# Three edits to a sixteen-layer kernel: quarter-array PV, a maximum from a copy, encoder products issued last

## The chip, the cores and the metric

The kernel runs on one core of a Trainium2 chip. The metric is device time in microseconds for the whole program, lower is better. TensorE is written PE, VectorE DVE, ScalarE ACT, GpSimd POOL and SyncE SP.

## The reference, cut to what matters

The input is 8 batches of 256 tokens with 128 features. Sixteen residual layers run one after the other, `x = x + layer(layernorm(x))`. The layers that the change touches are:

- layers 1 and 3, routed attention. Four groups times eight batches give 32 units. A router picks for each unit 128 query tokens and 64 key tokens. Eight heads of 64 features attend over the 64 keys and one learned null key with its null value; the result is projected to 128 features, weighted by the query's gate and added back at the tokens it came from.

```python
scores = q @ k.T * 64 ** -0.5            # 128 queries x (64 keys + the null key), 8 heads
p = softmax(scores)
out = (p[:, :64] @ v + p[:, 64] * v_null) @ w_out
```

- layers 2 (causal), 10 (no mask) and 14 (window of 64, with an output projection): attention with 16 heads of 8 features over 256 tokens, `softmax(q @ k.T * scale) @ v`.
- layers 13 and 15: a mixture of encoders. Two of four encoders are picked per batch, so each layer has 16 units. A unit is the same 16-head attention, a projection, a layer norm, a feed-forward of 128 to 512 to 128, and a second layer norm.

All matmuls of these layers are in float32.

## The kernel before, in words

Each layer is a stage with its own buffers and semaphores. Each engine runs one program written out in steps, in order, and semaphores tie the engines together.

**Routed stage** (`routed_attention_stage`, tiles `s1a_...` and `s3a_...`). A first part sorts the router's logits; its length is set by VectorE's top-k loop. Then step `i` works on unit `i` and finishes older units. TensorE issues in step `i`: the scores of unit `i` (`S`, L3259), the items of `RoutedPlan`, four turns of the probabilities of unit `i-1` (`PT`, L3270), PV of `i-2` (`OT`, L3282), the projection of `i-3` (`OUT`, L3293, and L3296 for the null value), and the scatter of `i-4` (`X`, L3305). The items are the value product of unit `i` (`v`, L3234), in three steps of four the front of the next group (gather: two items, L3212 and L3214; queries: four items, L3219; keys: two items, L3227), and the turn of the null probability of `i-1` (`pn`, L3241). All items write one ring of two banks, `F`:

```python
n = plan.number[it]
f = F[:, n % 2, :]
if n >= 2:
    pe.wait_ge(f_cp, n - 1)
```

so an item waits until the item two places before it has been copied out. ScalarE copies every item (the values at L3342, scaled by the gate), then takes the exponential of unit `i` (L3346), then copies `PT` and `OT`. VectorE's step is: maximum (L3412), subtraction (L3416), after the exponential the row sum (L3420) and reciprocal (L3423), then the copy of `OUT` (L3429), two additions into `x` from the scatter (L3446), and the placement matrix (L3405). POOL multiplies by the reciprocal and issues the indirect DMAs.

**Slot stages** (`slot_attention_stage`, and the same helpers in `encoder_stage`). `SlotPlan` gives 32 (or, in an encoder stage, 64) steps of four heads each. Scores are computed twice, once to find the row maxima and once turned, with the maximum subtracted in the product. Six PSUM banks in three pairs (`R`) rotate: the turned scores of step `u` overwrite the pair in which the first two heads' scores of step `u+1` stand, so they wait until VectorE has taken those maxima. TensorE's step `u` is: scores of `u+1` (L471), early items, PV of the step before (L520; two steps before with a mask), turned scores of `u` (L500), turns of the maxima of `u+1` (L534), turn of the output (L543), late items. The scores of `u+2` wait for the first exponential of `u` (L569), which needs the turned scores. Other products of the unit (queries and keys `qk`, values `v`, layer norm's turn `h`, and in the encoders `t`, `y`, `t1`, `f1`, `f2`, `f3`) share one bank `X` and are spread over four steps by two tables:

```python
early = {0: [("qk", 1)], 1: [("f1", -2)], 2: [("y", -1)], 3: [("f3", -2)]}
late = {0: [("t1", -2)], 1: [("t", -1)], 2: [("f2", -2)], 3: [("v", 1)]}
```

`qk` of the next unit is sent through DRAM (L409 store, L415 four loads) and must be back for the scores of the next unit's first step, issued in the fourth step of this one. SP's queue issues these and the loads of the encoders' weights in order.

## Time and profile before

| | |
|---|---|
| three runs | 3067.08, 3072.36, 3075.82 us; median 3072.36 |
| the profiled execution | 3062.8 us, its span 3061.1 us |
| mean granted clock of TensorE | 0.951 of full speed |
| busy share of the span | PE 88%, PE weight loads 59%, DVE 62%, ACT 45%, POOL 36% |
| routed stages, steady part | 397 to 622 and 860 to 1085 us |
| slot stages | 641 to 795 (causal), 1475 to 1641 (no mask), 2492 to 2637 us (window) |
| encoder stages | 2078 to 2450 and 2655 to 3040 us |

A stage is the stretch between the first and the last of its attention steps. In a timeline of TensorE the start of a row less the start of the row before is what the instructions of the row before cost; the busy time of a row includes the last matmul's run-out. float32 matmuls appear as two instructions each.

### The profile page before, as it was taken

The page shows a single profiled execution, that of the slowest core. Times are in us where ns is not written, and L with a number is a line of the kernel's source. Part 1 is how long each engine was busy: PE and PEld are TensorE (multiplying, and loading weights), DVE is VectorE, ACT ScalarE, POOL GpSimd, SP SyncE. Part 2 cuts the span into 40 slices and gives each one's busy share as a digit, 9 for nine tenths or more (in the row PEclk, how much of TensorE's full clock was granted, in tenths as well). Part 3 has the DMA queues.
Part 4 walks back from the last instruction along what each step waited for, and adds up shares of the span by engine and source line. Part 5 has one row for each costly group of instructions (what it writes and reads, how often), then busy time and mean ns, then how long its engine had stood idle before and what let it go on. Part 6 is the DMA issues. An engine that isn't in the chain of part 4 may idle for free. (4 is left out here: it accounts for less than half of the span.)

```text
span 3061.1 us, 62358 instructions
## 1 busy us (share of the span) xinstructions
PE 2707.2 (88%) x24181; PEld 1791.2 (59%) x24181; DVE 1910.4 (62%) x4325; ACT 1389.4 (45%) x2900; POOL 1094.8 (36%) x1448
## 2 busy tenths in 40 slices
PE   7899699978799977888788899997999989789997
PEld 2344367756467755566455677774666657456664
DVE  7888644556544566743675577765677746566764
ACT  5556144434244434423453355543555534355553
POOL 4788444324344323313112334330222246312222
PEclk9899799999789988988999999998999999999999
DMA  2000200001000001010111000002222201112221
GB/s 82 1 1 1 78 19 19 9 24 31 22 19 20 10 1 36 18 69 26 39 26 34 17 1 1 1 1 72 59 83 75 72 19 30 61 46 75 80 74 47
DMA packets 62498, 107.09 MB, mean 35 GB/s; under 512 B 8138, under 2 KB 47062, under 8 KB 61440
## 3 DMA queue, kind: packets, MB, share of 16 engines
q1 hardware_dynamic: 56832, 94.63, 10.3%
q0 software_dynamic: 5376, 8.47, 1.0%
q8 instruction: 197, 3.23, 0.4%
q14 instruction: 93, 0.76, 0.1%
HBM read 79.66 MB, written 23.86 MB: 34 GB/s over the span
## 5 line engine op out<-in xcount | busy, mean ns | idle before, releaser
L569 ACT ACTIVATE s_sT<-s_R 128x1024 f32<-128x1024 f32 (+2 forms) x448 | 415.6, 947 | 157.7 <-PE s_R L500 157.5
L604 DVE TENSOR_REDUCE s_negm<-s_R 128x4 f32<-128x1024 f32 x320 | 376.8, 1220 | 86.6 <-PE s_R L471 84.4
L471 PE MATMUL s_R<-s_qk 32*128 32x256 f32 (+2 forms) x3584 | 241.8, 382 | 92.2 <-ACT s_sT L569 66.8
L500 PE MATMUL s_R<-s_qA,s_qk 32*128 32x256 f32 (+2 forms) x3584 | 241.0, 382 | 20.9 <-DVE s_negm L604 12.6
L622 DVE TENSOR_TENSOR s_qA<-s_qk,s_OB 128x256 f32<-128x256 f32 x224 | 94.3, 421 | 264.6 <-PE s_OB L543 257.9
L471 PEld LDWEIGHTS s_R<-s_qk 32*128 32x128 f32 x3584 | 159.3, 185 | 142.6 <-issue 122.3
L520 PE MATMUL s_OB<-s_sT,s_v 128*32 128x256 f32 (+2 forms) x3584 | 224.5, 368 | 10.2 <-ACT s_sT L569 6.4
L500 PEld LDWEIGHTS s_R<-s_qA,s_qk 32*128 32x128 f32 x3584 | 163.2, 185 | 106.1 <-issue 102.8
L576 ACT ACTIVATE s_oc<-s_OB 128x256 f32<-128x256 f32 x224 | 85.8, 383 | 268.6 <-PE s_OB L520 264.3
L1519 POOL TENSOR_TENSOR s_pr<-s_pr,s_rinv 128x1024 f32<-128x1024 f32 x64 | 121.1, 1892 | 186.7 <-DVE s_rinv L1630 186.7
L2860 POOL TENSOR_TENSOR all_hT<-s0s_hs,s0s_cb 128x1024 f32<-128x1024 f32 x64 | 150.6, 2353 | 29.2 <-PE s0s_Y L2807 13.8
L520 PEld LDWEIGHTS s_OB<-s_sT,s_v 128*32 128x32 f32 x3584 | 94.1, 109 | 96.0 <-issue 33.2
L2886 DVE TENSOR_TENSOR_SCAN s0s_hs<-s0s_dA,s0s_dBu 128x1024 f32<-128x1024 f32 x64 | 146.1, 2283 | 0.9 <-POOL s0s_dBu L2848 0.9
L609 DVE TENSOR_REDUCE s_negm<-s_R 128x2 f32<-128x256 f32 (+2 forms) x256 | 116.4, 518 | 45.3 <-PE s_R L481 45.0
L585 POOL TENSOR_SCALAR_AFFINE_SELECT s_sT<-s_sT 128x512 f32<-128x512 f32 x128 | 81.2, 634 | 159.6 <-ACT s_sT L569 157.9
L2807 PE MATMUL s0s_Y<-all_hT,all_ident 128*128 128x512 f32 x256 | 125.2, 612 | 2.4 <-POOL all_hT L2860 2.4
L1195 POOL TENSOR_TENSOR s_veps<-s_mv,all_eps 128x2 f32<-128x2 f32 x64 | 16.6, 260 | 303.5 <-DVE s_mv L1403 303.5
L1603 ACT ACTIVATE s_pr<-s_S,s_negmax 128x256 f32<-128x256 f32 x256 | 117.4, 478 | 4.1 <-DVE s_negmax L1633 4.1
L534 PE MATMUL s_OB<-all_ident,s_negm 128*128 128x128 f32 x448 | 98.0, 300 | 2.8 <-DVE s_negm L604 2.5
L1633 DVE TENSOR_REDUCE s_negmax<-s_S 128x4 f32<-128x1024 f32 x64 | 78.3, 1223 | 29.5 <-PE s_S L1539 29.4
L1645 DVE COPY s_prT<-s_PT 128x1024 f32<-128x1024 f32 x64 | 78.3, 1224 | 22.8 <-PE s_PT L1568 22.8
L1611 ACT ACTIVATE s_v<-s_O 128x256 f32<-128x256 f32 x64 | 24.6, 384 | 147.1 <-PE s_O L1557 147.1
(613 smaller groups left out, 6263.0 us busy)
## 6 DMA issues: line engine op xcount, KB each, us to landing
s_wB<-enc_b SPq DMA_DIRECT2D x32, 962.5 KB, 4.8
s_scratch<-s_pk SPq DMA_DIRECT2D x58, 256.0 KB, 2.0
s_qk<-s_scratch SPq DMA_DIRECT2D x232, 64.0 KB
s_wA<-enc_a SPq DMA_DIRECT2D x32, 193.0 KB, 4.2
big<-moe SPq DMA_DIRECT2D x2, 2347.0 KB, 10.8
all_W<-weights SPq DMA_DIRECT2D x2, 2199.5 KB, 13.5
big<-routed SPq DMA_DIRECT2D x2, 2084.0 KB
s_returned<-s_back SPq DMA_DIRECT2D x2, 1024.0 KB
```

The lines of the kernel that those rows point to most:

```text
L471: last = pe.matmul(S[h][:, t * T:t * T + hi - lo], b.qk[rows, r % 2, 0, c, t * P:(t + 1) * P], b.qk[rows, r % 2, 1, c, lo:hi], start=(t == ...
L500: last = pe.matmul(b.R[:, a.turned_at(u, h // 2), :][:, h % 2, a.at(kt)], b.qk[rows, r % 2, 1, c, kt * P:(kt + 1) * P], b.qA[rows, u % 2, ...
L520: last = pe.matmul(b.OB[32 * h:32 * (h + 1), lo:hi], b.v[:, r % 2, kt, a.HP * c + h, :], b.sT[:, j % (a.lag + 1), h, a.at(kt)], start=(kt ...
L534: last = pe.transpose(b.OB[:, T + t * P:T + (t + 1) * P], b.negm[:, u % 2, t, :], g.ident[:])
L569: act.activation(b.sT[:, u % (a.lag + 1), 2 * p:2 * p + 2, 0:a.width], b.R[:, a.turned_at(u, p), 0:a.width], ACT.Exp).then_inc(s.expd, 1)
L604: ins = dve.tensor_reduce(b.negm[:, u % 2, :, at].rearrange("p t h -> p h t"), S.rearrange("p h (t k) -> p h t k", t=TT), AX_X, ALU.max, n ...
L609: ins = dve.tensor_reduce(b.negm[:, u % 2, t, at], S[:, :, t * T:t * T + hi - lo], AX_X, ALU.max, negate=True)
L1519: pool.tensor_tensor(p, p, rinv[:, u % 3, :, :].rearrange("p h t -> p (h t)").unsqueeze(2) .to_broadcast([P, 2 * TT, T]), ALU.mult).then_i ...
L1603: ins = act.activation(pr[:, u % 3, h, t, :], S[:, u % 2, h, t * T:(t + 1) * T], ACT.Exp, bias=negmax[:, u % 3, h, t:t + 1], accum_out=sum ...
L2807: last = pe.matmul(Y[:, m, :], g.ident[:], hc[:, j % 2, m, :], start=False, stop=(j % N == N - 1), skip_group_check=True)
L2860: pool.tensor_tensor(hc[:, q % 2, :, :], hs[:, q % 2, :, :], cb[:, q % 2, :].unsqueeze(1).to_broadcast([P, M, C]), ALU.mult)\
L2886: dve.tensor_tensor_scan(out=hs[:, q % 2, :, :].rearrange("p m c -> p (m c)"), data0=dA[:, q % 2, :, :].rearrange("p m c -> p (m c)"), dat ...
```

## The change

Three edits, of which the first has several parts.

1. Routed stages. PV alternates over the four 64x64 quarters of the array, with the output in two banks, where it used the two diagonal quarters. Values are stored less the null value, `v - v_null`, and the null value's projection is added once per query as a constant row (`nw`) when `OUT` is taken out; the turn of the null probability, its copy, its POOL product and the 8-row matmul L3296 go. The values' copy moves from ScalarE to VectorE, between the subtraction and the row sum. `OUT` and `X` share one bank, and the scatter is issued before the projection.
2. Slot stages (layers 2, 10, 14), `hold=True`. ScalarE copies the second head's scores to SBUF (`kept`); VectorE takes the maxima of head 0 from PSUM, of heads 2 and 3 from PSUM, of head 1 from the copy. The turned scores wait for head 0's maximum and the copy.
3. Encoder stages. Items move between the tables, early items are issued after PV, and ScalarE does the late items' copies after both exponentials.

```diff
-    early = {0: [("qk", 1)], 1: [("f1", -2)], 2: [("y", -1)], 3: [("f3", -2)]}
-    late = {0: [("t1", -2)], 1: [("t", -1)], 2: [("f2", -2)], 3: [("v", 1)]}
+    early = {0: [("t1", -2)], 1: [("t", -1)], 2: [("y", -1)], 3: [("v", 1)]}
+    late = {0: [("qk", 1)], 1: [("f1", -2)], 2: [("f2", -2)], 3: [("f3", -2)]}
...
                     if u + 1 < U:
                         slot_scores_pe(pe, g, a, b, u + 1)
+                    if 0 <= u - a.lag < U:
+                        slot_pv_pe(pe, a, b, u - a.lag)
                     for item in a.early(u):
                         other(item)
-                    if 0 <= u - a.lag < U:
-                        slot_pv_pe(pe, a, b, u - a.lag)
...
+                    if 0 <= u - a.lag < U:
+                        slot_out_act(act, a, b, u - a.lag)
                     for item in a.early(u):
                         other(item)
-                    if 0 <= u - a.lag < U:
-                        slot_out_act(act, a, b, u - a.lag)
                     if 0 <= u < U:
                         slot_exp_act(act, a, b, u, 0)
+                        slot_exp_act(act, a, b, u, 1)
                     for item in a.late(u):
                         other(item)
-                    if 0 <= u < U:
-                        slot_exp_act(act, a, b, u, 1)
```

In the encoders VectorE's addition of `f3` moves with its item to the end of the step. The slot stages:

```diff
+def slot_hold_act(act, a, b, u):
+    s = b.sems
+    act.wait_ge(s.scored, 2 * u + 1)
+    if u:
+        act.wait_ge(s.maxed, a.maxima * u)
+    act.activation(b.kept[:, 0:a.key_width], b.R[:, a.scores_at(u, 0), :][:, 1, 0:a.key_width], ACT.Copy)\
+       .then_inc(s.held, 1)
...
+def slot_max_dve(dve, a, b, u):
+    s = b.sems
+    pairs = [b.R[:, a.scores_at(u, p), :] for p in range(2)]
+    dve.wait_ge(s.scored, 2 * u + 1)
+    if a.maxima == 3:
+        slot_maxima_of(dve, a, b, u, (0,), pairs[0][:, 0:1, :]).then_inc(s.maxed, 1)
     else:
+        slot_maxima_of(dve, a, b, u, (0, 1), pairs[0]).then_inc(s.maxed, 1)
+    dve.wait_ge(s.scored, 2 * u + 2)
+    slot_maxima_of(dve, a, b, u, (2, 3), pairs[1]).then_inc(s.maxed, 1)
+    if a.maxima == 3:
+        dve.wait_ge(s.held, u + 1)
+        slot_maxima_of(dve, a, b, u, (1,), b.kept[:].unsqueeze(1)).then_inc(s.maxed, 1)
...
     if u + 1 < a.U:
-        pe.wait_ge(s.maxed, 2 * (u + 1) + 1)
+        pe.wait_ge(s.maxed, a.maxima * (u + 1) + 1)
+        if a.maxima == 3:
+            pe.wait_ge(s.held, u + 2)
...
                 for u in a.steps:
+                    if u + 1 < U:
+                        slot_hold_act(act, a, b, u + 1)
                     for item in a.early(u):
```

The routed stages:

```diff
-            if 0 <= i - 1 < self.UNITS:
-                items.append(("turn", i - 1))
...
                         if n >= 2:
-                            pe.wait_ge(f_cp, n - 1)
+                            old = plan.order[n - 2]
+                            if old[0] == "v":
+                                pe.wait_ge(v_cp, old[1] + 1)
+                            else:
+                                pe.wait_ge(f_cp, plan.copies[old] + 1)
...
                             for h in range(H):
-                                rows = slice((h % 2) * DH, (h % 2 + 1) * DH)
-                                c = h // 2
-                                last = pe.matmul(OT[rows, c * P:(c + 1) * P], v[rows, j % 3, c * DH:(c + 1) * DH],
+                                half, c = h % 2, h // 2
+                                rows, to = slice(half * DH, (half + 1) * DH), half ^ (c % 2)
+                                last = pe.matmul(OT[to * DH:(to + 1) * DH, c % 2, (c // 2) * P:(c // 2 + 1) * P],
+                                                 v[rows, j % 3, c * DH:(c + 1) * DH],
                                                  prT[rows, j % 2, c * P:(c + 1) * P], start=True, stop=True,
-                                                 skip_group_check=True)
+                                                 skip_group_check=True, tile_position=(half * DH, to * DH))
...
+                        j = i - 3
+                        if 0 <= j < U:
+                            s = plan.unit(j)[0]
+                            pe.wait_ge(oT_cp, j + 1)
+                            if j >= 1:
+                                pe.wait_ge(o_cp, j)
+                            if j >= 2:
+                                pe.wait_ge(added, TT * (j - 1))
...
+                    def values(u):
+                        n, s, c = plan.number[("v", u)], plan.unit(u)[0], columns(u)[1]
+                        dve.wait_ge(f_mm, n + 1)
+                        dve.scalar_tensor_tensor(out=v[:, u % 3, :], in0=F[:, n % 2, 0:256], scalar=sig[:, 1, c:c + 1],
+                                                 in1=g.big("r_nvb")[:, s * 256:(s + 1) * 256], op0=ALU.mult,
+                                                 op1=ALU.subtract).then_inc(v_cp, 1)
...
                                               ALU.subtract).then_inc(shifted, 1)
+                            values(i)
                             dve.wait_ge(expd, i + 1)
...
-                            dve.tensor_copy(o[:, j % 2, :], OUT[:, 0:D]).then_inc(o_cp, 1)
+                            dve.tensor_tensor(o[:, j % 2, :], OUT, nw[:, plan.unit(j)[0], :], ALU.add)\
+                               .then_inc(o_cp, 1)
...
                             dve.wait_ge(scattered, j + 1)
+                            dve.wait_ge(projected, min(j + 2, U))
```

The packed weights of the routed layers gain `r_nvb` (1024 columns) and `r_nvc` (16) and lose `r_nvT` (128); `nw` has 128 equal rows in place of one row per head.

## Rows read from the trace of the kernel before

**Rows 1.** Busy time by stage: routed (first), slot without mask, second encoder.

```profile
397.00:622.00 225.00, 222.51 (x1908) 161.82 (x1904) 121.72 (x296) 101.73 (x216) 92.95 (x128) 0.98 0.05 15
...
1475.00:1641.00 166.00, 137.20 (x1732) 84.85 (x1725) 115.32 (x234) 84.12 (x122) 22.05 (x40) 1.00 0.10 25
...
2655.00:3040.00 385.00, 349.89 (x3956) 232.28 (x3956) 250.45 (x549) 203.44 (x342) 89.24 (x151) 0.99 0.23 71
```

**Rows 2.** Timeline of TensorE, one routed step and the next.

```profile
481.94 1.11 PE L3259 MATMUL s1a_S<-s1a_kT,s1a_qT 64*128 64x65 f32 x16
...
483.56 0.33 PE L3212 MATMUL s1a_F<-all_ident,s_hq 128*128 128x128 f32 x1
...
484.21 0.33 PE L3212 MATMUL s1a_F<-all_ident,s_hq 128*128 128x128 f32 x1
...
485.44 1.09 PE L3282 MATMUL s1a_OT<-s1a_prT,s1a_v 64*64 64x128 f32 x16
...
486.46 1.16 PE L3293 MATMUL s1a_OUT<-big,s1a_oT 128*128 128x128 f32 x8
...
487.55 0.48 PE L3296 MATMUL s1a_OUT<-s_nw,s1a_pnT 8*128 8x128 f32 x2
...
488.60 1.11 PE L3259 MATMUL s1a_S<-s1a_kT,s1a_qT 64*128 64x65 f32 x16
...
490.23 3.80 PE L3219 MATMUL s1a_F<-s1a_sel,big 128*128 128x512 f32 x8
```

**Rows 3.** Timeline of TensorE, causal slot stage.

```profile
692.14 0.86 PE L520 MATMUL s_OB<-s_sT,s_v 128*32 128x256 f32 x16
...
692.93 0.94 PE L500 MATMUL s_R<-s_qA,s_qk 32*128 32x256 f32 x16
```

**Rows 4.** Timeline of VectorE, routed step.

```profile
488.07 0.29 DVE L3429 COPY s1a_o<-s1a_OUT 128x128 f32<-128x128 f32 x1 [1.19 <-PE s1a_OUT L3296]
...
488.78 0.61 DVE L3446 SCALAR_TENSOR_TENSOR all_x<-s1a_X,s_rcount,all_x 128x128 f32<-128x128 f32 x2 [0.42 <-PE s1a_X L3305]
...
489.76 0.70 DVE L3412 TENSOR_REDUCE s1a_mx<-s1a_S 128x8 f32<-128x520 f32 x1
...
490.50 0.70 DVE L3416 TENSOR_TENSOR s1a_ev<-s1a_S,s1a_mx 128x520 f32<-128x520 f32 x1
```

**Rows 5.** Waits in the routed stage, 450 to 550 us.

```profile
PEld s1a_F L3212 <- ACT s1a_v L3342: 0.9, 4, 0.2
```

**Rows 6.** Timeline, slot stage without mask, one plain step.

```profile
1554.29 1.15 PE L471 MATMUL s_R<-s_qk 32*128 32x256 f32 x16 [0.61 <-ACT s_sT L569]
...
1555.36 1.07 PE L520 MATMUL s_OB<-s_sT,s_v 128*32 128x256 f32 x16
...
1555.62 2.33 DVE L604 TENSOR_REDUCE s_negm<-s_R 128x4 f32<-128x1024 f32 x2
...
1556.95 1.15 PE L500 MATMUL s_R<-s_qA,s_qk 32*128 32x256 f32 x16 [0.52 <-DVE s_negm L604]
...
1559.29 1.15 PE L471 MATMUL s_R<-s_qk 32*128 32x256 f32 x16 [0.39 <-ACT s_sT L569]
```

**Rows 7.** Timeline of TensorE, first encoder, scores of four steps.

```profile
2231.67 1.15 PE L471 MATMUL s_R<-s_qk 32*128 32x256 f32 x16 [0.40 <-ACT s_sT L569]
...
2237.16 1.15 PE L471 MATMUL s_R<-s_qk 32*128 32x256 f32 x16 [0.40 <-ACT s_sT L569]
...
2240.95 0.44 PE L534 MATMUL s_OB<-all_ident,s_negm 128*128 128x128 f32 x2
...
2242.41 1.15 PE L471 MATMUL s_R<-s_qk 32*128 32x256 f32 x16
...
2248.81 1.15 PE L471 MATMUL s_R<-s_qk 32*128 32x256 f32 x16 [0.17 <-ACT s_sT L569]
```

**Rows 8.** Timeline of SyncE's queue, first encoder.

```profile
2229.34 0.33 SPq L409 DMA_DIRECT2D s_scratch<-s_pk  x1
```

**Rows 9.** DMA share and GB/s in a half microsecond.

```profile
2236.50:2237.00 0.50, 1.00 0.03 2
```

More of the change, by code:

```diff
@@ L188, with __init__ @@
     QUERIES = {None: ((0, 256), (0, 256)), "causal": ((0, 256), (128, 256)), "window": ((0, 192), (128, 256))}
-    def __init__(self, units, early, late, extra, mask=None, first=()):
+    def __init__(self, units, early, late, extra, mask=None, first=(), hold=False):
         self.units, self.U, self.mask = units, units * self.NC, mask
         self.lag = 1 if mask is None else 2
+        self.maxima = 3 if hold else 2
         self.steps = range(-1, self.U + extra)
@@ L470, in slot_scores_pe @@
             rows = slice(32 * h, 32 * (h + 1))
-            last = pe.matmul(S[h][:, t * T:t * T + hi - lo], b.qk[rows, r % 2, 0, c, t * P:(t + 1) * P],
+            last = pe.matmul(S[h][:, a.keys_at(t)], b.qk[rows, r % 2, 0, c, t * P:(t + 1) * P],
                              b.qk[rows, r % 2, 1, c, lo:hi], start=(t == 0), stop=(a.mask is None and t == TT - 1),
@@ L643, in slot_attention_stage @@
         early[3], late[2] = [("y", -1)], [("t", -1)]
-    a = SlotPlan(B, early, late, 4, mask, [("h", 0), ("qk", 0), ("v", 0), ("h", 1)])
+    a = SlotPlan(B, early, late, 4, mask, [("h", 0), ("qk", 0), ("v", 0), ("h", 1)], hold=True)
     U, NC = a.U, a.NC
@@ L767, in _ @@
                     if u + 1 < U:
-                        for p in range(2):
-                            slot_max_dve(dve, a, b, u + 1, p)
+                        slot_max_dve(dve, a, b, u + 1)
                     for item in a.early(u):
@@ L1408, in _ @@
                     if u + 1 < U:
[L1409 to L1410 removed]
+                        slot_max_dve(dve, a, b, u + 1)
                     for item in a.early(u):
@@ L1460, in _ @@
                                                  op1=ALU.add).then_inc(unit_done, 1)
+                    for item in a.late(u):
+                        what, r = item
+                        if what == "f3":
+                            dve.wait_ge(x1b_ready, r + 1)
+                            if r:
+                                dve.wait_ge(unit_done, r)
+                            dve.wait_ge(s.x_mm, a.number[item] + 1)
+                            dve.tensor_tensor(r2[:], b.X[:, 0:T].rearrange("p (t n) -> p t n", t=TT),
+                                              x1b[:, r % 2, :, :], ALU.add).then_inc(r2_ready, 1)
+                            dve.wait_ge(r2_ready, r + 1)
+                            dve.sem_inc(s.x_used, 1)
                     if (r := at_step(u, 3, -3)) is not None and r % 2 and r // 2 < leave:
@@ L2936, in __init__ @@
                     items += self.front(nxt, ("gather", "q", "k")[i % self.NB - 1])
-            if 0 <= i - 1 < self.UNITS:
-                items.append(("turn", i - 1))
             self.steps.append(items)
-        self.number = {item: n for n, item in enumerate(item for s in self.steps for item in s)}
+        self.order = [item for s in self.steps for item in s]
+        self.number = {item: n for n, item in enumerate(self.order)}
+        self.copies = {item: n for n, item in enumerate(item for item in self.order if item[0] != "v")}
     @staticmethod
@@ L3185, in copied @@
             def copied(*item):
-                return plan.number[item] + 1
+                return plan.copies[item] + 1
             with nc.Block() as block:
@@ L3305, in _ @@
                                 last = pe.matmul(X[:, h * D:(h + 1) * D], sqT[:, j % 4, h * P:(h + 1) * P],
-                                                 o[:, j % 2, :], start=True, stop=True)
+                                                 o[:, j % 2, :], start=True, stop=True, skip_group_check=True)
                             last.then_inc(scattered, 1)
+                        j = i - 3
[6 more added lines that the diff above has]
+                                pe.wait_ge(added, TT * (j - 1))
+                            for c in range(4):
+                                at = (c % 2) * T + (c // 2) * P
+                                last = pe.matmul(OUT, oT[:, j % 2, at:at + P], wo[:, (4 * s + c) * P:(4 * s + c + 1) * P],
+                                                 start=(c == 0), stop=(c == 3), skip_group_check=True)
+                            last.then_inc(projected, 1)
                 @block.scalar
```

119 lines of the change are left out of this document (44 added, 75 removed).

## Prediction, written before the change was run

> **What bounds the kernel now.** I read the busy table by stage first. The change touches seven of sixteen stages, about 1700 of 3061 us. In the routed stages PE is busy 222.5 of 225 us at a granted clock of 0.98, DVE only 121.7 [rows 1]: every microsecond taken from PE's program there is a microsecond, until another engine is late. The slot stage without a mask is different: PE 137 and DVE 115 of 166 us, so no engine is full, and a loop of waits sets the step. The encoder has PE 350 of 385 us. Next I read PE's timeline of one routed step, start to start [rows 2], and the same of VectorE [rows 4]. For the loops I read one plain slot step with its waits [rows 6] and the starts of the scores over the steps of an encoder unit [rows 7].
>
> **Routed stages: what PE loses.** 32 units in each of two stages.
> - PV: 16 instructions from 485.44 to 486.46, 1.02 us [rows 2]. Two quarters work at a time, so these are eight groups of two. The 16 instructions at L3219 take 3.80/8 = 0.475 us for 512 columns with the run-out, some 0.11 us per 128 columns, and eight groups at 0.11 plus the entry are the 1.02. With four quarters there are four groups: 0.44 us less per unit, if all four run together. No row shows quarters mixed this way. Bounds: 0, if a quarter in the same rows has to wait, and 0.44. Four slices in one direction do run together: in the causal stage 16 PV instructions, half of them of 256 columns, go by in 0.79 us, 49 ns each [rows 3], against 107 ns and more for one alone. I take 0.44.
> - The Trainium skill, page "TensorE: Matmul & The Clock Gate", section "Wait — 56ns, not 53.3ns?", speaks against this: with instructions decoded by the sequencer each matmul costs about 62 ns however short. 16 times that is the 1.0 us of today, and the quarters would save nothing. The 49 ns of the causal row lie below it, so the trace disagrees and I keep the full term.
> - The turn of the null probability is one instruction of 128 columns: 0.11 us.
> - From the first projection to the next scores now: 488.60 - 486.46 = 2.14 us: eight full instructions with a slow entry and exit (1.09), the 8-row pair (0.41), the scatter's four with another entry (0.64). The new order has twelve full instructions with one entry and exit: 1.09 + 4 x 0.11 = 1.53. That is 0.60 us less.
> - Together 1.15 us per unit, 64 units: **-74 us**.
>
> **Routed stages: what comes back.** The values' copy is now behind VectorE's maximum and subtraction, and an item waits for the copy of the one two before it. Today ScalarE frees the values' bank in time: 0.9 us of such waits in 100 us, at most 0.2 [rows 5]. After the change:
> - The maximum starts 1.16 us after the first score matmul today (489.76 - 488.60). `OUT` is now the last thing before the scores. Its taking out started 0.31 us after the last matmul of its group (488.07 against 487.76), which is 0.11 after the next scores start. Then 0.29 for it, and 0.98 from the first addition to the maximum [rows 4]: the maximum starts at 1.38.
> - Subtraction at 1.38 + 0.74, its end 0.70 later, values about 0.45 (nearest rows: 0.41 for L3405's kind, a 256-column operation; I take a little more for two inputs), a hop of 0.05: bank free at 3.32.
> - The second gather item could start at 484.21 - 481.94 = 2.27, the second query item at 1.62 + 0.95 = 2.57, the second key item at about 2.5. Waits: 1.05, 0.75, 0.80; 2.6 us in a group of four, seven groups, two stages: +36. In the first eight steps VectorE has two more additions of 0.3 behind it: +4. Bounds: 0, should the copy not be late, and 1 us more per wait (42 waits, +42) should VectorE run behind. I take **+40**.
> - VectorE itself: 121.7/32 = 3.8 us per unit plus 0.45. The shortest step (no front) is 6.66 less two gather items of 0.65, 5.36; it becomes 4.2. VectorE's 4.25 just reaches it: +1.
> - ScalarE loses 0.47 + 0.25 us per unit, POOL a product of 0.2. Neither is late today, so nothing. The copy of `OUT` becomes an addition of the same size, 0. The load grows by 912 columns, 0.47 MB; it lies under the top-k loop, and without that cover it would be 1 to 2 us.
> - Net **-33 us**.
>
> **Slot stages.** In a plain step the turned scores start 1556.95 - 1554.29 = 2.66 us after the scores, having waited 0.52 for VectorE; the next scores follow 2.34 later [rows 6]. The two-head maximum takes 1.17 (2.33 for two). One of 520 elements takes 0.70 [rows 4], and ScalarE's copy, which takes part beside it, about 0.6. So the wait falls to the end of PV, 1.07 + 1.0 = 2.07, and the step from 5.0 (4.88 where no layer norm stands before it) to 4.4: 0.5 us. But only one step in four can use it: with an item ahead of PV the turned scores were not waiting for VectorE, and in the fourth step the turns of the maxima, now 0.1 us later because three reduces take 2.45 instead of 2.33, with `h` behind them fill the gap. 8 x 0.5 = 4. With masks the maxima are shorter: 8 x 0.35 and 8 x 0.3. **-9 us**; if the copy gains nothing and all 96 steps get 0.1 longer, +10.
>
> **Encoders.** Two steps in four now take 5.49 us (2237.16 - 2231.67), the third 5.25, the fourth 6.40 [rows 7]. All have a product between scores and turned scores, and then 2.3 us to the next scores in which PE rests 0.4 at the least [rows 7]. Behind the turned scores a product fills that rest, and it needs no change of array shape. `f2` shows the price: 2242.41 - 2240.95 = 1.46 from the maxima's turns to the next scores with a late product of four instructions of 256 columns. The first two steps get the maxima's turns at 3.7 (2.66 + 1.08) and a late `qk` or `f1` of the same size: 3.7 + 1.46 = 5.16, -0.33 each. The third keeps its pair, 0. The fourth has `v` early and `f3` late, 16 instructions of 0.11 instead of four of 0.22: 3.79 + 1.46 + 0.9 = 6.15, -0.25. That is 0.91 us per unit, 14 units with all items, two stages: -25; in the first encoder the next layer's norm work makes VectorE late in every other unit, +2. **-23 us**.
> - `qk` of the next unit moves from some 3 us into the first step to about 6.7: turned scores, two exponentials and then the copies, which ScalarE now does last. From the store's issue to the end of the loads is 7.4 to 7.7 us (2229.34 to 2236.5 or 2237.0) [rows 8, 9], so the data is there at 14.3, and the scores want it at 5.16 + 5.16 + 5.25 = 15.6. It is hidden with 1.3 us to spare. SP's queue holds the loads of the next weights behind it; they aren't wanted for a unit.
>
> **Sum.** -33 - 9 - 23 = **-65 us**. The profiled execution, 3062.8 us (span 3061.1), would become 2998. It lies 10 us below the median of the runs; from the median, 3072.4 - 65 = **3007 us**.
>
> **Rivals.**
> - The quarters run in pairs (bound 0): 64 x 0.44 = 28 us come back, 3035. For it: no row shows them. Against it: [rows 3].
> - The values' copy isn't late: VectorE takes it earlier than I think, all 40 us stay, 2967. Against it: its place in VectorE's program behind two operations of 0.7 us.
> - VectorE runs behind: `OUT` is now taken out at the end, and each wait is 0.7 us longer: 42 x 0.7 = +29, 3036. For it: 4.25 us of work against 4.2.
> - `qk` lands late: one microsecond in 28 units, 3035. For it: only 1.3 us to spare, and weights loads start while it lands.
> - The other side: the same wait behind VectorE becomes the routed stages' bound. To undo 65 us it must be 65/42 = 1.55 us longer than my 0.95; at 2.2 the time is 3100. It would take VectorE being a whole half step behind. Against it: query and key steps give VectorE 2 to 4 us to catch up.
>
> **How the numbers follow.** Forecast 0.48; quarters in pairs 0.12; copy not late 0.10; VectorE behind 0.11; `qk` late 0.09; two or three of these together, back to where it was, 0.05; the other side 0.05. A measurement of this kernel can't tell 0.3%, 9 us, from no change. Faster 0.90, same 0.05, slower 0.05. The range runs from the copy that isn't late to beyond the single rivals near 3035, to 3045, with 2970 below. The forecast's own range is 2990 to 3022.
>
> **What would show it.** Right: PV's 16 instructions in 0.6 us; from the first scatter to the next scores 1.53; the second item of each front waiting 0.7 to 1.1 us for VectorE's new values line, the largest new wait on PE; the short routed step near 4.3 us, the gather step near 5.5 plus its wait; plain slot steps of 4.4; encoder steps of 5.16, 5.16, 5.25 and 6.15. Wrong: PV still about 1 us, a wait of the scores for the loads of `qk`, gaps of PE before the probabilities' turns, or a lower granted clock where PE now rests.

## The result, and the profile after

The changed kernel took 3016.09 us (median, 3015.27 to 3018.5) beside 3073.15 for the kernel before on the same chip: a ratio of 0.9818, 95% interval 0.9801 to 0.9835, 57 us between the medians. The forecast was 3007 (range 2970 to 3045). The two profiled executions differ by 44 us only (3062.8 and 3018.5, spans 3061.1 and 3016.8). The 13 us between are the choice of executions: the one of before lies 10 us below its median, that of the changed kernel 2 above. Single profiles differ in parts that no edit touches as well: the stretch from the last scores of the second routed stage to the first of the slot stage without a mask took 405.6 us in the profile of before, 413.5 in that of after, and 404 to 412 in the experiments. The steady steps repeat to 0.01 us from profile to profile.

The busy times of the changed kernel's page:

```profile
PE 2647.1 (88%) x23955; PEld 1745.4 (58%) x23989; DVE 1944.5 (64%) x4549; ACT 1397.8 (46%) x2868; POOL 1086.0 (36%) x1384
```

Its timeline of TensorE, the same routed steps as [rows 2]:

```profile
486.03 0.33 PE L3248 MATMUL s1a_F<-all_ident,s_hq 128*128 128x128 f32 x1 [0.76 <-DVE s1a_v L3438]
...
487.05 0.67 PE L3316 MATMUL s1a_OT<-s1a_prT,s1a_v 64*64 64x128 f32 x16
487.65 0.71 PE L3328 MATMUL s1a_OX<-s1a_o,s1a_sqT 128*128 128x128 f32 x4
488.20 1.06 PE L3341 MATMUL s1a_OX<-big,s1a_oT 128*128 128x128 f32 x8
489.18 1.11 PE L3291 MATMUL s1a_S<-s1a_kT,s1a_qT 64*128 64x65 f32 x16
...
490.80 1.13 PE L3255 MATMUL s1a_F<-s1a_sel,big 128*128 128x512 f32 x2
492.22 2.94 PE L3255 MATMUL s1a_F<-s1a_sel,big 128*128 128x512 f32 x6 [0.29 <-DVE s1a_v L3438]
```

PV takes 0.60 us to the next row, where [rows 2] have 1.02, and from the scatter to the next scores it is 489.18 - 487.65 = 1.53, where it was 2.14. The second gather item waits 0.76 us for VectorE's values. The changed kernel's waits from 450 to 550 us (us in total, times, longest), as [rows 5]:

```profile
PEld s1a_F L3248 <- DVE s1a_v L3438: 4.7, 4, 1.7
...
PEld s1a_F L3255 <- DVE s1a_v L3438: 4.5, 4, 1.1
...
PEld s1a_F L3263 <- DVE s1a_v L3438: 2.1, 3, 0.7
```

Its timeline of VectorE in the gather step, as [rows 4]:

```profile
484.15 0.70 DVE L3446 TENSOR_REDUCE s1a_mx<-s1a_S 128x8 f32<-128x520 f32 x1
484.88 0.70 DVE L3450 TENSOR_TENSOR s1a_ev<-s1a_S,s1a_mx 128x520 f32<-128x520 f32 x1
485.50 0.47 DVE L3438 SCALAR_TENSOR_TENSOR s1a_v<-s1a_F,s_sig,big 128x256 f32<-128x256 f32 x1
```

The maximum starts 1.16 us after the scores and the values' copy 0.62 after the subtraction; the bank is free at about 486.0. The first eight steps look different. TensorE in the early gather step of the changed kernel:

```profile
426.35 1.11 PE L3291 MATMUL s1a_S<-s1a_kT,s1a_qT 64*128 64x65 f32 x16
...
431.22 0.47 PE L3248 MATMUL s1a_F<-all_ident,s_hq 128*128 128x128 f32 x1 [2.59 <-DVE s1a_v L3438]
...
432.12 1.06 PE L3303 MATMUL s1a_PT<-all_ident,s1a_pr 128*128 128x128 f32 x4
433.12 1.13 PE L3316 MATMUL s1a_OT<-s1a_prT,s1a_v 64*64 64x128 f32 x16
```

VectorE in the same step:

```profile
427.06 1.53 DVE L3469 SCALAR_TENSOR_TENSOR all_x<-all_W,s_missed,all_x 128x128 f32<-128x128 f32 x2
428.51 0.60 DVE L3483 SCALAR_TENSOR_TENSOR all_x<-s1a_OX,s_rcount,all_x 128x128 f32<-128x128 f32 x2
...
430.69 0.48 DVE L3438 SCALAR_TENSOR_TENSOR s1a_v<-s1a_F,s_sig,big 128x256 f32<-128x256 f32 x1
```

POOL beside it, the product of the probabilities with the reciprocal:

```profile
427.07 1.04 POOL L3415 TENSOR_TENSOR s1a_pr<-s1a_ev,s1a_rsum 128x512 f32<-128x512 f32 x1 [1.14 <-DVE s1a_rsum L3458]
```

Busy times and granted clock (the third value from the right) while it waits, right after, over the rest of the step and in the next:

```profile
428.70:431.20 2.50, 0.00 (x0) 0.00 (x0) 2.43 (x6) 0.46 (x1) 1.64 (x2) 0.94 0.09 26
431.20:432.20 1.00, 0.98 (x5) 0.98 (x6) 0.00 (x0) 0.00 (x0) 0.00 (x0) 0.50 0.21 66
432.20:435.70 3.50, 3.50 (x33) 2.78 (x31) 0.90 (x2) 2.10 (x4) 1.10 (x2) 0.70 0.02 5
435.80:437.30 1.50, 1.50 (x21) 1.13 (x20) 1.42 (x6) 0.00 (x0) 1.20 (x2) 1.00 0.00 0
```

The additions of the null token take 1.53 us for two ahead of the maximum, the values' copy starts 430.69 - 426.35 = 4.34 us after the scores, and the gather item waits 2.59. The first of the two additions alone takes 1.20 us, and it ends 0.15 after POOL's product (428.11); where no product of POOL runs beside them they take 0.33 to 0.41 each. Near the end of the wait TensorE's granted clock fell to half, for 3.4 us: the turns of the probabilities took 1.06 us in place of 0.60, PV 1.13 in place of 0.67.

TensorE's timeline of a plain slot step after the change (compare [rows 6]):

```profile
1522.00 1.15 PE L481 MATMUL s_R<-s_qk 32*128 32x256 f32 x16 [0.61 <-ACT s_sT L581]
...
1524.12 1.15 PE L512 MATMUL s_R<-s_qA,s_qk 32*128 32x256 f32 x16
...
1526.45 1.15 PE L481 MATMUL s_R<-s_qk 32*128 32x256 f32 x16 [0.16 <-ACT s_sT L581]
```

And the scores of an encoder unit (compare [rows 7]):

```profile
2201.47 1.15 PE L481 MATMUL s_R<-s_qk 32*128 32x256 f32 x16
...
2206.55 1.15 PE L481 MATMUL s_R<-s_qk 32*128 32x256 f32 x16
...
2211.64 1.15 PE L481 MATMUL s_R<-s_qk 32*128 32x256 f32 x16
...
2216.88 1.15 PE L481 MATMUL s_R<-s_qk 32*128 32x256 f32 x16
...
2223.05 1.15 PE L481 MATMUL s_R<-s_qk 32*128 32x256 f32 x16
```

The plain step fell from 4.88 or 5.0 to 4.45; the turned scores start 2.12 us after the scores (2.66 before). The encoder's steps are 5.08, 5.09, 5.24 and 6.17, a sum of 21.58 where it was 22.63. But in some units the scores wait for `qk`. SyncE's queue for a good unit (compare [rows 8]):

```profile
2208.12 0.33 SPq L419 DMA_DIRECT2D s_scratch<-s_pk  x1
2210.14 2.85 SPq L425 DMA_DIRECT2D s_qk<-s_scratch  x4
```

The same for a bad one:

```profile
2384.23 0.33 SPq L419 DMA_DIRECT2D s_scratch<-s_pk  x1
2387.84 2.84 SPq L425 DMA_DIRECT2D s_qk<-s_scratch  x4
```

And its scores on TensorE:

```profile
2394.69 1.15 PE L481 MATMUL s_R<-s_qk 32*128 32x256 f32 x16 [1.64 <-DMA s_qk<-s_scratch]
```

The loads are issued when the store has completed: 2.02 us after it in the one, 3.61 in the other. There the scores wait 1.64. The DMA view shows an instruction fetch beside the slow store (packets, MB, share; then KB and us to landing):

```profile
q8 instruction: 1, 0.02, 2.5%
...
s_scratch<-s_pk SPq DMA_DIRECT2D x1, 256.0 KB, 3.6
```

Beside the fast one it shows none:

```profile
s_scratch<-s_pk SPq DMA_DIRECT2D x1, 256.0 KB, 2.0
```

Stage by stage, from the first scores to the last in the profiles (us):

| stage | before | after | measured | forecast |
|---|---|---|---|---|
| routed, layers 1 and 3 | 210.7, 210.1 | 198.6, 199.3 | -12.1, -10.8 | -33 for both |
| causal slot | 142.3 | 138.7 | -3.6 | -3 |
| slot without mask | 155.9 | 149.3 | -6.6 | -4 |
| window slot | 132.1 | 134.8 | +2.7 | -2 |
| encoders, layers 13 and 15 | 360.7, 357.7 | 354.5, 348.7 | -6.2, -9.0 | -23 for both |

The seven stages add up to 46 us less, near the 44 by which the two profiled executions differ, and not the 57 of the medians.

### The profile page after: what moved, and what is told of

Same layout as the page of the kernel before. It is cut to its first block and busy times, and to the rows that moved or that the text cites. A ratio compares the mean times of both kernels' runs of the same rounds, so it can differ in the third digit from the quotient of the medians.

```text
span 3016.8 us, 62251 instructions
## 1 busy us (share of the span) xinstructions
PE 2647.1 (88%) x23955; PEld 1745.4 (58%) x23989; DVE 1944.5 (64%) x4549; ACT 1397.8 (46%) x2868; POOL 1086.0 (36%) x1384
## 3 DMA queue, kind: packets, MB, share of 16 engines
q0 software_dynamic: 5376, 8.47, 1.0%
## 5 line engine op out<-in xcount | busy, mean ns | idle before, releaser
L581 ACT ACTIVATE s_sT<-s_R 128x1024 f32<-128x1024 f32 (+2 forms) x448 | 402.8, 945 | 187.0 <-PE s_R L512 186.8
L623 DVE TENSOR_REDUCE s_negm<-s_R 128x4 f32<-128x1024 f32 (+1 forms) x320 | 359.5, 1166 | 102.5 <-PE s_R L481 101.2
L627 DVE TENSOR_REDUCE s_negm<-s_R 128x1 f32<-128x128 f32 (+5 forms) x256 | 92.8, 425 | 41.8 <-PE s_R L491 41.5
L546 PEld LDWEIGHTS s_OB<-all_ident,s_negm 128*128 128x128 f32 x448 | 45.1, 141 | 83.0 <-DVE s_negm L623 60.8
## 6 DMA issues: line engine op xcount, KB each, us to landing
big<-moe SPq DMA_DIRECT2D x2, 2347.0 KB, 10.8
```

The source lines that it names most:

```text
L546: last = pe.transpose(b.OB[:, T + t * P:T + (t + 1) * P], b.negm[:, u % 2, t, :], g.ident[:])
L581: act.activation(b.sT[:, u % (a.lag + 1), 2 * p:2 * p + 2, 0:a.width], b.R[:, a.turned_at(u, p), 0:a.width], ACT.Exp).then_inc(s.expd, 1)
L623: return dve.tensor_reduce(b.negm[:, u % 2, :, at].rearrange("p t h -> p h t"), S[:, :, 0:a.key_width].rearrange("p h (t k) -> p h t k", t ...
```

## The experiments

Each kernel's ratio is to the kernel before, run on the same chip; the changed kernel's is 0.9818. Differences between two kernels are differences of their ratios, times 3070 us. Stage times are those of one profile for each kernel. Twelve kernels ran.

**pairs.** PV on the two diagonal quarters again, the rest as changed (the order of the projection's packed weights and of the null values follows, not shown).

```diff
-half, c = h % 2, h // 2
-rows, to = slice(half * DH, (half + 1) * DH), half ^ (c % 2)
+rows, to = slice(half * DH, (half + 1) * DH), half
```

> The changed kernel with each product of PV back on the two diagonal quarters of the array (rows and columns of the same half), the projection's weights and the null values in the order that fits; everything else stays, the two output banks too. My theory, four quarters work side by side: PV's 16 instructions go from 0.60 us back to about 1.0, the steps of the routed stages get 0.4 us longer, and the time is 64 x 0.44 = 28 us longer (20 to 30). The rival, that the quarters run in pairs and PV became shorter by something else (the second bank, the order): PV stays at 0.60 us and the time within 3 us.

3030.17 us, 0.9867 (0.9849 to 0.9886): 15 us slower than the changed kernel. Its timeline:

```profile
487.77 1.09 PE L3316 MATMUL s1a_OT<-s1a_prT,s1a_v 64*64 64x128 f32 x16
488.79 0.71 PE L3328 MATMUL s1a_OX<-s1a_o,s1a_sqT 128*128 128x128 f32 x4
```

PV is back at 1.02 us. Every steady step is 0.42 us longer (4.34 to 4.76, 6.19 to 6.62, 8.47 to 8.90, 6.67 to 7.09), the two stages 10.9 and 9.9. The whole time misses the 20 to 30 us that were expected, and is 6 us nearer to the changed kernel than these two stages say; in this profile the stretch of 413.5 us named above took 407.8, the window stage 3.9 us less and the encoders 5.5 more. Parts outside the edit differ by such amounts from profile to profile. In the routed steps the rival is out: with both banks kept, PV took 1.02 us on two quarters and 0.60 on four.

**nulls.** The null token's additions behind the values' copy, under the exponential.

```diff
                             values(i)
+                            if i < B:
+                                for t in range(TT * i, TT * i + TT):
...
                             dve.wait_ge(expd, i + 1)
...
-                        if i < B:
-                            for t in range(TT * i, TT * i + TT):
...
```

> The changed kernel with the two additions of the null token (first eight steps of each routed stage) moved on VectorE from ahead of the next maximum to behind the values' copy, where VectorE otherwise waits for the exponential. Theory: in the changed kernel they take 1.4 us of each early step and hold up the maximum and the values' copy behind it, so that the second item of a front waits 1.8 to 2.6 us where it waits 0.7 later on, and after such a wait PE runs for a while at the lower clock. Moved, the early gather step falls from 9.4 us to 6.2, the other early steps by 0.5 to 2.5, some 7 us for each of two stages: 14 us faster in all. Rival, that the early steps are long for another reason (the gathers' transfers arriving, the softmax starting from nothing): within 3 us, and the early gather step stays at 9.4.

2995.80 us, 0.9755 (0.9739 to 0.9772), 19 us faster than the changed kernel. The routed stages took 192.1 and 191.8 us (6.5 and 7.5 less); the early gather step fell from 9.42 to 6.35, and no steady step changed. The expected 14 us are there; the other 5 lie outside these stages. The edit did two things at once. The additions left VectorE's way to the values' copy, and they left the place beside POOL's product. VectorE in the early gather step:

```profile
425.07 0.61 DVE L3457 SCALAR_TENSOR_TENSOR all_x<-all_W,s_missed,all_x 128x128 f32<-128x128 f32 x2
```

The 32 additions of both stages took 11.0 us together, in the changed kernel 20.1. No run moved the one without the other, so how the 14 us divide between the order and the 9 us of slower additions isn't shown.

**mid.** The values' copy between maximum and subtraction.

```diff
 dve.tensor_reduce(mx[:, i % 2, :, :], s4, AX_X, ALU.max).then_inc(maxed, 1)
+values(i)
 dve.wait_ge(maxed, i + 1)
 ...
-values(i)
 dve.wait_ge(expd, i + 1)
```

> The changed kernel with the values' copy placed between the maximum and the subtraction on VectorE instead of behind both. Theory: the bank comes free 0.7 us earlier, which is the whole wait of the second items of the fronts (0.69 us for a gather, 0.56 for q and k, in steady steps), so some 12 us in the steady steps of both stages and as much again in the first eight, 15 to 25 us faster. The softmax starts 0.47 us later, which costs nothing as long as the probabilities are there for their turns in the next step. Rival: the later softmax makes PE wait ahead of the probabilities' turns in the short steps (4.34 us), 0.3 to 0.5 us in most of 64 steps, which eats the gain: between 5 us faster and 15 slower.

2988.38 us, 0.9737 (0.9716 to 0.9758), 25 us faster than the changed kernel. The stages took 187.6 us each (11.0 and 11.7 less). The steady steps fell from 6.19, 8.47, 6.67 to 5.63, 7.92, 6.12, the short one stayed at 4.34. The early gather step stayed at 9.11: that one belongs to nulls. The later softmax cost nothing in the steady steps; the first step of a stage grew from 2.74 to 3.00.

**both.** The two edits together.

> The changed kernel with both edits of VectorE's program in the routed stages: the values' copy between maximum and subtraction, and the two additions of the null token behind the subtraction, under the exponential. Alone the first made a routed stage 11.4 us shorter than in the changed kernel and the second 7.0. Theory: they take away different waits (the steady ones of the second front items, and those of the first eight steps), but in the first eight steps they overlap by the 0.55 us of each steady wait, 2 to 3 us in a stage: 30 to 36 us faster than the changed kernel in all, a stage of 182 to 184 us, and an early gather step of about 5.7 us. Rival, that the early steps then wait for the probabilities or for the gathers' transfers: no more than the first edit alone, 24 us, and an early gather step that stays above 8.

2974.02 us, 0.9695 (0.9673 to 0.9717), 38 us faster than the changed kernel; the stages took 180.7 and 181.0, 17.9 and 18.3 less, nearly the sum of the two. The early gather step is 5.73 us long:

```profile
424.87 0.33 PE L3248 MATMUL s1a_F<-all_ident,s_hq 128*128 128x128 f32 x1 [0.29 <-DVE s1a_v L3438]
...
425.37 0.60 PE L3303 MATMUL s1a_PT<-all_ident,s1a_pr 128*128 128x128 f32 x4
```

**routed_only.** The kernel before with the routed part alone.

> The kernel before with the routed stages' part of the change alone; encoders as before and no copied head in the slots. My sum had 33 us for it (74 less on PE, 40 back in waits, 1 for VectorE). The profile of the changed kernel shows its two routed stages 12.1 and 10.8 us shorter: 23 us. Theory: 0.9925 of the kernel before (0.990 to 0.995). Rival, that the change gains outside the stages' steps as well (the values' and weights' loads, the front): 0.989 or less.

3043.90 us, 0.9921 (0.9906 to 0.9936): 24 us faster than before. The stages took 198.6 and 199.3 us, as in the changed kernel.

**enc_only.** The kernel before with the encoders' part alone.

> The kernel before with the encoders' part of the change alone (the long products behind the turned scores, both exponentials together); the routed stages and the slot stages as before the change. My sum had 23 us for it; the steady steps of the changed kernel show 1.05 us per unit, 29 us for 28 units, less the waits for the loads of qk, 9 us in its profile, and less some 3 us in the first steps. Theory: 12 to 20 us faster than the kernel before, and waits of the scores for the loads of qk as in the changed kernel. Rival, that these waits come from elsewhere (another stage's edit shifting the transfers): none of them here, and 23 us or more faster.

3039.89 us, 0.9904 (0.9877 to 0.9931): 29.5 us faster than before, more than I expected, with an interval from 21 to 38. Its profile shows 349.8 and 353.5 us for the encoders, 15.1 less than before, with steps of 5.08, 5.08, 5.25 and 6.17 and many waits for the loads of `qk`. Much of the difference is again which executions were profiled: the one of enc_only lies 6.5 us above its median, that of before 7 below the median of the runs beside it, and the two differ by 16. Between the profile's 15 and the median's 29 the runs do not decide, nor between the theory and the rival's 23 or more, though the waits for the loads, which the rival would have gone, are there.

**qbetween.** ScalarE copies `qk` between the two exponentials; the products stay late.

```diff
                         slot_exp_act(act, a, b, u, 0)
+                    copied = [item for item in a.late(u) if item[0] == "qk"]
+                    for item in copied:
+                        other(item)
+                    if 0 <= u < U:
                         slot_exp_act(act, a, b, u, 1)
                     for item in a.late(u):
-                        other(item)
+                        if item not in copied:
+                            other(item)
```

> The changed kernel with the copies of the encoders' qk taken by ScalarE between the two exponentials (as before the change) instead of behind them; the products stay where they are. Theory: in the changed kernel the scores of a new unit wait for the loads of qk whenever a store or load is slow, some 9 us over the two encoders (0.1 to 1.7 us in about half of the units); 0.9 us earlier most of it goes: 5 to 9 us faster, if the second exponential, now 0.9 us later, is still there for PV. Rival, that these waits come from the store's own length and return whatever the start: within 3 us. Rival, that the later exponential makes PV wait: slower by 0.4 us in each of 32 units, 13 us.

3021.26 us, 0.9837 (0.982 to 0.9854), 6 us slower than the changed kernel. The theory's shorter waits and the second rival both came true. The waits for the loads went (0.3 us in the steady units, 7.8 in the changed kernel), and every second step of a unit rose from 5.08 to 5.91 us, 0.83 where 0.4 was expected. The encoders took 11.6 us more, the window stage 3.9 less. TensorE in such a step:

```profile
2206.71 1.15 PE L481 MATMUL s_R<-s_qk 32*128 32x256 f32 x16
2208.72 1.07 PE L532 MATMUL s_OB<-s_sT,s_v 128*32 128x256 f32 x16 [0.86 <-issue]
```

ScalarE's copies and its second exponential there:

```profile
2206.87 0.47 ACT L458 ACTIVATE s_pk<-s_X,s_bqs 128x256 f32<-128x256 f32 x1 [0.40 <-ACT s_bqs L1346]
...
2207.60 1.02 ACT L581 ACTIVATE s_sT<-s_R 128x1024 f32<-128x1024 f32 x1
```

PV starts 2.01 us after the scores in place of 1.08. ScalarE also lost 0.40 us of its own between the bias and its use; in the changed kernel it has no such gap there.

**enctab.** One step earlier for the encoders' `f` items, `qk` a unit ahead.

```diff
-    late = {0: [("qk", 1)], 1: [("f1", -2)], 2: [("f2", -2)], 3: [("f3", -2)]}
-    a = SlotPlan(UNITS, early, late, 14)
+    late = {0: [("f1", -2)], 1: [("f2", -2)], 2: [("f3", -2)], 3: [("qk", 2)]}
+    a = SlotPlan(UNITS, early, late, 14, None, [("qk", 0), ("v", 0), ("qk", 1)])
...
                 other(("v", 0))
+                other(("qk", 1))
```

> The changed kernel with the encoders' late items one step earlier (f1, f2, f3 behind the turned scores of the first three steps) and the qk product of the unit after the next in the fourth step's place; the first two units' qk are made ahead of the loop. The work of each unit on PE is the same, and the store and the loads of qk have a whole unit more. Theory: the scores no longer wait for the loads of qk, 5 to 9 us over both encoders, the four steps become 5.08, 5.08, 6.17 and 5.25 us (the same sum of 21.57), and the first unit's wait for its loads gets shorter by up to 6 us an encoder: 9 to 20 us faster. Rival, that the stores are slow because of what else is on the queue then: the waits for the loads stay. Rival, that f3 behind y makes a third step in which VectorE is late: the sum of four steps grows by 0.3 us or more, 5 to 10 us slower.

3001.03 us, 0.9783 (0.976 to 0.9805), 11 us faster than the changed kernel. The encoders took 347.6 and 346.5 us (6.9 and 2.2 less) with steps of 5.08, 5.08, 6.17, 5.25. The waits are gone; the first unit's is not: its fourth step still took 11.8 us in the first encoder and 9.9 in the second.

**encsp.** In addition, the second unit's `qk` ahead of the weights.

```diff
+                slot_store_sp(sp, a, b, scratch, 1)
                 for r in range(3):
                     load(r, "b")
                 for r in range(UNITS):
-                    if r + 1 < UNITS:
+                    if 1 <= r < UNITS - 1:
                         slot_store_sp(sp, a, b, scratch, r + 1)
```

> The kernel of the run enctab with one more edit: the store and loads of the second unit's qk stand ahead of the three loads of encoder weights (962 KB each) in SP's program instead of behind them. Theory: in the changed kernel the fourth step of each encoder takes 11 to 14 us because these loads come behind 2.9 MB of weights; ahead of them they land in time, and the fourth step falls to about 6 us: 6 to 8 us faster than enctab for each encoder, 12 to 16 in all, unless the first weights are then late in the second unit. Rival, that the fourth step is long for another reason (the weights themselves): within 3 us of enctab.

2981.59 us, 0.9723 (0.9699 to 0.9747), 18 us faster than enctab; the encoders took 338.9 and 337.3 us, 8.7 and 9.2 less. The first unit's fourth step took 4.88 us in both. SyncE's queue at the start of the first encoder in the changed kernel:

```profile
2065.17 2.59 SPq L1200 DMA_DIRECT2D s_wB<-enc_b  x3
2068.49 0.33 SPq L419 DMA_DIRECT2D s_scratch<-s_pk  x1
2077.36 2.84 SPq L425 DMA_DIRECT2D s_qk<-s_scratch  x4
```

The scores that wait for these loads:

```profile
2084.24 2.09 PE L481 MATMUL s_R<-s_qk 32*128 32x256 f32 x16 [6.72 <-DMA s_qk<-s_scratch]
```

The queue in encsp:

```profile
2052.71 0.43 SPq L419 DMA_DIRECT2D s_scratch<-s_pk  x1
2054.84 3.01 SPq L425 DMA_DIRECT2D s_qk<-s_scratch  x4
2059.28 2.60 SPq L1200 DMA_DIRECT2D s_wB<-enc_b  x3
```

Behind 2.9 MB of weights the store took 8.9 us to complete, ahead of them 2.1. All waits of the scores' line for these loads (us, times), changed kernel:

```profile
  DMA s_qk<-s_scratch: 65.8, 46
```

The same in encsp:

```profile
  DMA s_qk<-s_scratch: 2.1, 2
```

This view adds up matmuls and weight loads. TensorE's matmuls alone waited 13.3 and 10.1 us in the encoders of the changed kernel, 14.8 of it in the fourth steps of the two first units, and not at all in those of encsp.

**nohold.** The changed kernel without the copied head: `hold=True` goes.

> The changed kernel without the copied head in the three slot stages (maxima of two heads at a time, straight from the scores' bank). My sum had 9 us for the copied head: 4 in the stage without a mask, 3 in the causal, 2 in the window. The profiles show 6.6, 3.6 and about 1, when the window stage's first wait for its loads is left out: 11 us slower than the changed kernel, a ratio of 0.985 to the kernel before. Rival, that the extra wait of 2.4 us at the window stage's start, seen in the changed kernel, belongs to the copied head: then it is gone here and only 8 us are lost. A second rival, nothing: the plain steps were set by something else, within 3 us.

3010.21 us, 0.9810 (0.9795 to 0.9825): not slower. Yet its causal stage took 142.1 us and the one without a mask 155.9, 10 us more together, and the window stage 131.9. In this profile the 10 us are made up by the encoders, 348.5 and 347.5 us or 7 less than in the changed kernel, with only 1.6 us of waits for the loads of `qk` in their steady units, and by the window stage, 3 less. These waits (each unit's third step less the shortest one, both encoders) were 7.8, 12.2, 11.7, 7.9, 13.4, 10.8 and 1.6 us in the changed kernel, pairs, nulls, mid, both, enc_only and nohold. All seven have the same encoder code. Each has one profile, so whether the waits go with the kernel or with the execution isn't shown.

**all.** both and encsp together.

> The changed kernel with the edits of the runs both and encsp together: VectorE's order in the routed stages, the encoders' late items one step earlier with qk a unit ahead, and the second unit's qk ahead of the weights on SP's queue. They touch different stages. Against the kernel before, both stood at 0.9695 and encsp at 0.9723, the change at 0.9818; if the gains add up: 0.9818 - 0.0123 - 0.0095 = 0.960, some 2947 us. Rival, that a part of both gains was one thing (the window stage's first wait for its loads, which was 3 us longer in some runs than in others): 0.963 or more.

2950.26 us, 0.9612 (0.9596 to 0.9629), 119 us faster than the kernel before and the fastest of all. The gains added up to within 4 us. Its window stage took 135.3 us, so the rival's late load is in it.

**all_nohold.** The same without the copied head.

> The kernel of the run all without the copied head in the three slot stages. In the run nohold, which took the head out of the changed kernel, the causal stage and the stage without a mask were 3.4 and 6.7 us longer in the profile, yet the kernel was not slower (0.9810 against 0.9818), and the two encoders' waits of the scores for the loads of qk were 7 us shorter there than in the changed kernel's profile. Theory: the head is worth what its stages show, 10 us less up to 3 us for the window stage's start, and what hid it in nohold were those waits, which differ from kernel to kernel (1.6 to 13 us over both encoders in the seven kernels with the change's encoders). In this kernel they are gone, so its time is 7 to 10 us longer than that of all: a ratio to the kernel before of 0.9635 to 0.9645 where all has 0.9612. Rival: what the head gives in its stages is taken back somewhere else whatever the encoders do: within 3 us of all.

2962.49 us, 0.9647 (0.9634 to 0.9661), 0.35% or 11 us slower than all (4 to 17 with both intervals). So with the encoders' waits out of the way the copied head has a gain in the whole time, and the rival of none is out. The profiles show less: without the head the causal stage and the one without a mask took 3.2 and 6.6 us more, the window stage 3.3 less (132.0), the encoders 2.6 less, and the two spans differ by 6.3.

## Why the prediction came out as it did

The sign and the main mechanisms were right, and the time came out 9 us above the forecast. Part of that closeness is luck: by the stages of the profiles the change takes away 46 us of the forecast 65, and the 11 us between 46 and the medians' 57 go with the choice of the profiled executions and weren't forecast.

- **PE's term in the routed stages, -74.** Four quarters together: 0.44 forecast, 0.42 measured (pairs, and 1.02 to 0.60). New order: 0.60 forecast, 0.61 measured (2.14 to 1.53). The short step fell by 1.09 us where the sum had 1.15; over the 62 steps between first and last scores that is 67 us. The prediction's price of 0.475 us was read off a row of eight instructions, not 16; the price itself stands. Beside this stands a figure that argued against the quarters. The Trainium skill, page "TensorE: Matmul & The Clock Gate", section "Wait — 56ns, not 53.3ns?", has about 62 ns for each matmul when the sequencer decodes, and gives it for hardware decode switched off. 16 in 0.60 us are 37.5 ns, so that bound did not hold here; no run shows how this program's matmuls are decoded.
- **The waits for the values' copy, +40.** 67 us less the 23 measured leave 44, close to the forecast, but only because two misses cancel. In steady steps the copy comes sooner than I said: gather, query and key steps give back 1.09 less their gains of 0.47, 0.58 and 0.59, 0.62 + 0.50 + 0.50 = 1.6 us per group in place of 2.6, because the maximum starts 1.16 us after the scores, not 1.38, and the copy does not wait for the subtraction's whole 0.70. The later five groups of each stage give back 18 us in all, where 26 were forecast; the first two (steps 1 to 8) give back 25, where 14 were. The last 2 us are first steps, in which nothing got shorter. The step that failed is "two more additions of 0.3 behind it: +4". The price was wrong: of two additions ahead of a maximum the pair took 0.6 to 1.5 us, since in seven of the eight steps one of them ran beside POOL's product and lasted until 0.15 after it. Waits of 0.8 to 2.6 us follow, and with the longest the clock drops. nulls gives back 14 us of it in the stages.
- **VectorE's cover, +1.** The short step came out at 4.34 (4.3 forecast), but TensorE waits for nothing in it: 4.34 is the 5.43 of before less PE's 1.09. The +1 for VectorE did not show.
- **Slots, -9.** By the stages -7.5; by all against all_nohold 11, within 4 to 17. "Only one step in four can use it" was wrong: the fourth step, with `h`, fell too (5.01 to 4.59). The window stage gives 1.2 us when the second unit's loads are in time (130.9 against 132.1) and loses 2.7 when they are not. That happened in the profile of the changed kernel and in four of the eight experiments with the head, and in none of the five kernels without it; whether the head has a part in it, and why the loads are late in some, is open.
- **Encoders, -23.** 5.16, 5.16, 5.25 and 6.15 were forecast, 5.08, 5.08, 5.25 and 6.17 measured: 1.05 us per unit, not 0.91, 29 us for 28 units. The stages show 15: 7.8 went to the waits below, and the first two units of the two encoders got 4 us longer in all; the other 2 were not traced to a step. The rival "`qk` lands late" came true in part beside it: "from the store's issue to the end of the loads is 7.4 to 7.7 us" was read off one unit, and the store alone varies from 2.0 to 3.6, more than the 1.3 us to spare. It cost 7.8 us here, 1.6 to 13.4 in other profiles. enctab, which gives the loads a unit more, shows 0.3.
- **The other rivals** did not occur: no quarters in pairs (pairs), no copy that is in time (0.76 us of wait in the gather step), no steady VectorE lateness (short steps of 4.34), and nowhere 2.2 us of wait beyond the first eight steps.

## What to carry to other kernels

When work moves to another engine's in-order program, look at the first steps as well as the steady one: the costliest waits here were behind operations that run in eight steps of thirty-two. Price an operation by a row in which the same engines run beside it: an addition of 0.34 us took 1.2 beside POOL's product. Give a transfer through DRAM slack by its slowest instance and by what stands ahead of it on its queue, not by one row. Before judging one edit by the whole time, look for a wait elsewhere that differs between profiles of the same code; here the encoders took 7 us less in the very profile that should have shown a loss of 10.

## What was not expected of the hardware

- The completion of the same 256 KB store varied from 2.0 to 3.8 us with no weights ahead of it on its queue, and took 8 to 10 behind 2.9 MB of weights. Over the profiles of all fourteen kernels, window and encoder stages, I took the time from a store's issue to the issue of its first load. A store in whose first 1.9 us a packet of an instruction fetch of 8 KB or more was under way took over 2.15 us in 112 of 202 cases, and one without in 17 of 316. Without the 22 stores behind weights it is 106 of 196 against 1 of 300. That would also explain why profiles of the same encoder code show waits of 1.6 to 13.4 us: the fetches fall elsewhere. It is an association read from the traces; no run changed the fetches.
- An addition of VectorE (`x` from the null token, 128x128) that started while POOL's product of 128x512 ran, or together with it, ended 0.14 to 0.15 us after the product, in all 124 such cases of the fourteen profiles, and took up to 1.20 us. Where the product started 0.17 us after the addition (60 cases), the addition took 0.30. The 260 with no such product beside them took 0.33 to 0.41. Here too no run changed that alone.
- Sixteen float32 matmul instructions of 128 columns on four 64x64 quarters went by in 0.60 us, 37.5 ns each, against 64 ns in pairs.
- After 2.59 us without a matmul the granted clock was 0.50 (1.2 GHz) for 3.4 us and 1.00 again by the next scores; the same wait in the second routed stage (2.58) was followed by the same 3.4 us. Waits of 0.76 us (486.03) and 1.80 us (418.83) left it at 1.00: PV took its 0.67 after the first.
